# Rotary embedding in a six-layer stage: the halves of a head swapped by a shuffle of partitions on VectorE, in place of a second projection on TensorE

## The reference, cut to what matters

```python
NL, D, H, DFF = (6, 128, 16, 512)
HD = D // H
def _rope(x):
    half = HD // 2
    ...
    x1, x2 = (x[..., :half], x[..., half:])
    return jnp.concatenate([x1 * cos - x2 * sin, x1 * sin + x2 * cos], axis=-1)
for i in range(NL):
    xn = _adaln(x, noise_emb, n1_w[i], n1_b[i])
    qkv = xn @ qkv_w[i].T
    ...
    q = _rope(q.reshape(B, L, H, HD)); k = _rope(k.reshape(B, L, H, HD))
    x = x + _attn(q, k, v, src_mask).reshape(B, L, D) @ so_w[i].T
    xn = _adaln(x, noise_emb, n2_w[i], n2_b[i])
    q = _rope((xn @ cq_w[i].T)...); k = _rope((context @ ck_w[i].T)...); v = (context @ cv_w[i].T)
    x = x + _attn(q, k, v, ctx_mask).reshape(B, L, D) @ co_w[i].T
    ...                     # feed-forward part
```

## Time and profile before

| what | value |
|---|---|
| median of 3 runs | 8145.55 us (8137.73 to 8151.84) |
| the profiled execution's own time | 8119.01 us |
| its span, first to last instruction | 8117.1 us |
| TensorE busy | 6394.4 us (79%) |
| VectorE busy | 5039.5 us (62%) |
| ScalarE busy | 2829.9 us (35%) |
| GpSimd busy | 831.3 us (10%) |
| mean granted TensorE clock | 0.829 |

### The profile page before, as it was taken

One profiled execution on the slowest core, in us unless ns is written; L12 is line 12 of the kernel. 1 busy time (PEld: TensorE's weight loads), 2 busy tenths in 40 slices (PEclk: granted clock), 3 DMA queues, 4 the chain that ended last, 5 costly groups with the idle time before them and its releaser, 6 DMA issues. The chain is left out here.

```text
span 8117.1 us, 210088 instructions
## 1 busy us (share of the span) xinstructions
PE 6394.4 (79%) x89378; PEld 4794.1 (59%) x89401; DVE 5039.5 (62%) x17947; ACT 2829.9 (35%) x4816; POOL 831.3 (10%) x803
## 2 busy tenths in 40 slices
PE   4444589989866698988978868888888888888875
PEld 3333467766643388888856645556556555565653
DVE  6777855455456666666643367577575775756742
ACT  2121133333322311111111135555455554555541
POOL 1114400000000100000000011111110111101100
PEclk7667799999988855555579989999999999999986
DMA  1000000000000000000000000000000000000000
GB/s 31 1 2 1 27 1 1 1 1 1 1 4 0 3 4 4 4 4 4 4 22 0 0 18 2 7 6 2 10 2 4 8 2 10 2 2 10 2 4 10
DMA packets 61243, 45.06 MB, mean 6 GB/s; under 512 B 22521, under 2 KB 56125, under 8 KB 60227
## 3 DMA queue, kind: packets, MB, share of 16 engines
q1 hardware_dynamic: 60355, 32.26, 1.5%
HBM read 30.14 MB, written 2.10 MB: 4 GB/s over the span
## 5 line engine op out<-in xcount | busy, mean ns | idle before, releaser
L368 DVE TENSOR_REDUCE peak<-ps 128x8 f32<-128x1024 f32 (+1 forms) x832 | 816.8, 1023 | 267.1 <-PE ps L290 266.3
L410 ACT ACTIVATE e<-ps,H_lowT_c 77x1024 f32<-77x1024 f32 x384 | 405.6, 1105 | 259.9 <-PE ps L314 259.9
L410 ACT ACTIVATE e<-ps,H_lowT_s 128x1024 f32<-128x1024 f32 x384 | 407.0, 1111 | 248.5 <-PE ps L314 248.5
L328 PEld LDWEIGHTS ps<-e,H_vt 128*32 128x32 f32 (+1 forms) x12288 | 319.8, 112 | 255.5 <-ACT e L410 140.9
L328 PE MATMUL ps<-e,H_vt 128*32 128x128 f32 (+1 forms) x12288 | 432.9, 281 | 23.6 <-DVE xs L388 17.7
L314 PE MATMUL ps<-H_qr,H_km 32*128 32x128 f32 (+1 forms) x12288 | 424.6, 277 | 0.0
L314 PEld LDWEIGHTS ps<-H_qr,H_km 32*128 32x128 f32 (+1 forms) x12288 | 410.2, 170 | 15.4 <-issue 2.2
L1838 PE MATMUL ps<-F_hp,F_encW 128*128 128x1 bf16 (+2 forms) x12288 | 363.4, 166 | 24.7 <-issue 22.4
L1868 PE MATMUL ps<-F_eT,F_ctxp 77*128 77x1 f16 (+1 forms) x12288 | 375.4, 165 | 1.7
L418 ACT ACTIVATE oT<-ps 128x512 f32<-128x512 f32 x416 | 248.4, 597 | 365.9 <-PE ps L328 365.9
L2216 POOL TENSOR_TENSOR H_rstd<-H_veps,neghalf 128x4 f32<-128x4 f32 (+1 forms) x146 | 160.8, 1101 | 2076.3 <-DVE H_veps L2212 2076.3
(11 more groups left out here) (602 smaller groups left out, 14394.4 us busy)
## 6 DMA issues: line engine op xcount, KB each, us to landing
G_w<-in_L_ffn_w SPq DMA_DIRECT2D x16, 256.0 KB
H_f<-in_L_xcond_f_w SPq DMA_DIRECT2D x12, 256.0 KB
H_nw<-in_L_xcond_n_w SPq DMA_DIRECT2D x21, 128.0 KB, 2.1
A_cond<-in_cond SPq DMA_DIRECT2D x1, 2048.0 KB
out_x<-x_all SPq DMA_DIRECT2D x1, 2048.0 KB, 8.7
ctx_rows<-in_ctx SPq DMA_DIRECT2D x1, 1232.0 KB
D_wq<-in_L_xcond_attn_wq SPq DMA_DIRECT2D x2, 512.0 KB
D_wk<-in_L_xcond_attn_wk SPq DMA_DIRECT2D x2, 512.0 KB
```

The source lines that it names most:

```text
L328: last = nc.tensor.matmul(ps[PAD_COLS * s:PAD_COLS * (s + 1), FLAT, r * S:(r + 1) * S], vt_of(u)[0:keys, QUAD * r + s, :], e[0:keys, half, ...
L368: last = nc.vector.tensor_reduce(peak[:, HL * half:HL * (half + 1)], view, AX.X, ALU.max, negate=True)
L410: nc.scalar.activation(e[0:keys, half, :], ps[0:keys, AGAIN[half]:AGAIN[half] + 2, :].rearrange("p b t -> p (b t)"), ACT.Exp, bias=low(u) ...
```

## The change

`rotate` reads one bank instead of two. VectorE first copies the projection out of PSUM with its partitions permuted (a stream shuffle, by the list SWAP, which exchanges partitions 0 to 3 with 4 to 7 within each head of eight, and in the same way in every block of 32), then multiplies the unpermuted projection by the cosine table, waits for the shuffle's own semaphore, and multiplies the permuted copy by the sine table in place. `project` issues one product instead of two, into banks that now alternate with the group, and so waits for the rotation four jobs back instead of two. The four permuted weight matrices, their SBUF tiles and their DMAs are gone (two of the eleven ahead of each layer, two of the eleven within it).

```diff
-                            def project(r, g, i, a, b, src):
+                            def project(r, g, i, m, src):
                                 k, n = job(r, g, i), tokens(r, i)[1]
-                                if g:
-                                    pe.wait_ge(sem["rope_done"], k - 1)
-                                for bank, m in ((2 * i, a), (2 * i + 1, b)):
-                                    last = nc.tensor.matmul(ps[:, bank, 0:n], w[m][:], src, start=True, stop=True)
-                                last.then_inc(sem["q_done"], 1)
+                                if g >= 2:
+                                    pe.wait_ge(sem["rope_done"], k - 3)
+                                nc.tensor.matmul(ps[:, 2 * i + g % 2, 0:n], w[m][:], src, start=True, stop=True).then_inc(sem["q_done"], 1)
...
-                                project(SELF, g, 0, "q_w", "qs_w", xnT2[g % 2][:])
+                                project(SELF, g, 0, "q_w", xnT2[g % 2][:])
...
-                                project(CROSS, g, 1, "ck_w", "cks_w", mine)
+                                project(CROSS, g, 1, "ck_w", mine)
...
                                 if k >= 2:
                                     dve.wait_ge(sem["table_ready"], k - 1)
-                                for bank, table, t in ((2 * i, cosT, ta), (2 * i + 1, sinT, tb)):
-                                    last = nc.vector.tensor_tensor(t[:, k % 2, 0:wide].rearrange("p (u t) -> p u t", u=U),
-                                                                   ps[:, bank, 0:wide].rearrange("p (u t) -> p u t", u=U),
-                                                                   table[:, 0:n].unsqueeze(1).broadcast_to([D, U, n]), ALU.mult)
-                                last.then_inc(sem["rope_done"], 1)
+                                by_batch = lambda t: t.rearrange("p (u t) -> p u t", u=U)
+                                over = lambda table: table[:, 0:n].unsqueeze(1).broadcast_to([D, U, n])
+                                src, kept, swapped = ps[:, 2 * i + g % 2, 0:wide], ta[:, k % 2, 0:wide], tb[:, k % 2, 0:wide]
+                                nc.vector.stream_shuffle(swapped, src, SWAP).then_inc(sem["halves_swapped"], 1)
+                                nc.vector.tensor_tensor(by_batch(kept), by_batch(src), over(cosT), ALU.mult)
+                                dve.wait_ge(sem["halves_swapped"], k + 1)
+                                nc.vector.tensor_tensor(by_batch(swapped), by_batch(swapped), over(sinT), ALU.mult).then_inc(sem["rope_done"], 1)
...
+                        SWAP = [HD * (i // HD) + (i + HD // 2) % HD for i in range(32)]
-                        LATER = 16 * 11
+                        LATER = 16 * 9
```

More of the change, by code:

```diff
@@ L46 @@
     "hid_done", "hid_ready", "ffn_done", "ffn_added", "gate_done", "gate_ready",
-    "upd_done", "upd_ready", "expert_done", "expert_ready", "x_ready", "gram_done",
+    "halves_swapped", "upd_done", "upd_ready", "expert_done", "expert_ready", "x_ready", "gram_done",
     "peaks_turned", "half_peaked", "shift_ready", "again_done", "o_read", "o_flipped",
@@ L2157, in stage_layers @@
                 y_all = sb("H_y", [S, B, D], scope=st)
-                square = ["q_w", "qs_w", "k_w", "ks_w", "v_w", "cqs_w", "cks_w"]
+                square = ["q_w", "k_w", "v_w"]
                 w = {n: sb("H_" + n, [D, D], scope=st) for n in square}
@@ L2261, in first_loads @@
                 def first_loads(l):
-                    out = [(w[n][:], of_layer(l, "L3_" + n, "a p n -> p (a n)")) for n in ("q_w", "qs_w", "k_w", "ks_w", "v_w")]
+                    out = [(w[n][:], of_layer(l, "L3_" + n, "a p n -> p (a n)")) for n in ("q_w", "k_w", "v_w")]
                     for i in range(3):
@@ L2271, in later_loads @@
                     out = [(w[n][:], of_layer(l, "L3_xcond_" + n, "a p n -> p (a n)")) for n in ("so_w", "ck_w", "cq_w", "cv_w", "co_w")]
-                    out += [(w[n][:], of_layer(l, "L3_" + n, "a p n -> p (a n)")) for n in ("cks_w", "cqs_w")]
                     out += [(f2b_raw[:], dram["L3_xcond_f2_b"][bass.ds(l, 1)].rearrange("a n -> (a n)").partition_broadcast(3)),
@@ L2406, in _ @@
                                 pe.wait_ge(sem["xnT_ready"], g + 1)
-                                project(SELF, g, 0, "q_w", "qs_w", xnT2[g % 2][:])
+                                project(SELF, g, 0, "q_w", xnT2[g % 2][:])
                                 if g + 1 < NG:
                                     turn(SELF, g + 1)
-                                project(SELF, g, 1, "k_w", "ks_w", xnT2[g % 2][:])
+                                project(SELF, g, 1, "k_w", xnT2[g % 2][:])
                                 if g == 1:
@@ L2429, in _ @@
                                 pe.wait_ge(sem["xnT_ready"], NG + g + 1)
-                                project(CROSS, g, 0, "cq_w", "cqs_w", xnT2[g % 2][:])
+                                project(CROSS, g, 0, "cq_w", xnT2[g % 2][:])
                                 if g + 1 < NG:
@@ L2808 @@
         arrays["L3_xcond_" + name] = arrays["L3_xcond_" + name].transpose(0, 2, 1)
-    swap = np.arange(D).reshape(NH, 2, HD // 2)[:, ::-1, :].reshape(-1)
     qkv = arrays["L3_xcond_qkv_w"]
     arrays["L3_q_w"], arrays["L3_k_w"], arrays["L3_v_w"] = qkv[:, :, 0:D], qkv[:, :, D:2 * D], qkv[:, :, 2 * D:]
-    arrays["L3_qs_w"] = arrays["L3_q_w"][:, :, swap]
-    arrays["L3_ks_w"] = arrays["L3_k_w"][:, :, swap]
-    arrays["L3_cqs_w"] = arrays["L3_xcond_cq_w"][:, :, swap]
-    arrays["L3_cks_w"] = arrays["L3_xcond_ck_w"][:, :, swap]
-    for name in ("L3_q_w", "L3_qs_w", "L3_k_w", "L3_ks_w", "L3_v_w", "L3_xcond_n1_w", "L3_xcond_n2_w", "L3_xcond_n3_w",
+    for name in ("L3_q_w", "L3_k_w", "L3_v_w", "L3_xcond_n1_w", "L3_xcond_n2_w", "L3_xcond_n3_w",
                  "L3_xcond_n1_b", "L3_xcond_n2_b", "L3_xcond_n3_b"):
```

## The result

The kernel after takes 8171.3 us (median of 10 runs, 8159.6 to 8205.6) against 8142.3 (10 runs, 8119.6 to 8159.3). The ratio is 1.0041, interval 1.0025 to 1.0057: 33 us slower (20 to 46). The profiled execution took 8177.6 us, its span is 8175.8, 58.7 more than the span before. VectorE is busy for 5147.0 us (+107.5), TensorE for 6335.6 (-58.8).

A forecast was written before the change was run, and what follows sets the result against it. SELF was taken as a ring through VectorE and TensorE with VectorE idle 1.27 us a group, CROSS as both full. SELF -1.37 and CROSS +6.74 us a layer gave +32, the clock +18: 8196 us, range 8164 to 8232.

The forecast's parts named there:

- The price of the shuffle: On VectorE, each rotation's added shuffle takes a step of 0.70 us at 512 columns, 0.49 at 308.
- Start: Up to a stretch's first normalisation: 1.70 us a layer gained in SELF, 0.45 lost in CROSS.
- Ring: SELF, first to last normalisation, through VectorE and TensorE in turn: 30.00 us a layer against 28.96, a loss of 1.04.
- Tail: After a stretch's last normalisation: SELF gains 0.47 us a layer, plus about 0.24 for earlier value rows; CROSS loses 0.45.
- Groups: CROSS, first to last normalisation: 26.63 us a layer against 20.79, +5.84, with a group at 5.15.
- The clock: TensorE, less busy, falls to half clock; VectorE waits in three of eight SELF groups: +18 us, bounds 0 and 52.
- The rule against the change: In SELF, the new sine multiplication may have to wait out GpSimd's add: sum 6 us higher, held by the range.
- The clock stays up: Rival: TensorE keeps its clock in both stretches, leaving +32 us, 8178 us; chance 0.14.
- The shuffle apart from its neighbours: Rival: on VectorE the shuffle overlaps no neighbour, a step of 0.90 us: +87 us, 8233 us; chance 0.12.
- the fast copy: Rival: on VectorE the shuffle runs as a fast copy, step 0.35 us: -15 us, 8131 us; chance 0.04.
- Normalisation freed: Rival: normalisation gets out from beside GpSimd's add, step 1.98 to about 1.04 us: -18 us, 8128 us; chance 0.03.
- Half of it: Rival: VectorE has overlooked slack in CROSS, only +10 us, 8156 us; chance 0.05.

The follow-up runs named there:

- g: The kernel after without the shuffle, the sine multiplication reading the projection unpermuted: 8076.5 us against 8138.9 for before, ratio 0.9928.
- b: The kernel before with the shuffle and single product in the SELF projections alone: 8143.9 us against 8138.9 for before, ratio 1.0010.
- c: The kernel before with the shuffle and single product in the CROSS projections alone: 8174.5 us against 8127.4 for before, ratio 1.0056.
- a: The kernel after with two spare products per group on TensorE whose results nobody reads: 8159.8 us, ratio to before 1.0025.
- h1: The kernel after, with GpSimd's add of a group's second rotation waiting for the normalisation of group g+2: 8129.5 us against 8127.4 for before.
- early cosine: The kernel before, each product signalling by itself, so the cosine multiplication begins when the first bank is written: 8096.9 us against 8127.4.
- late add: GpSimd's second add of a group waits for group g+2's normalisation: 8129.5 us on after (h1), 8081.9 on before with early cosine.
- r: The kernel before with early cosine and late add, and q in SELF with one product and a shuffle: 8059.4 us against 8129.3 for before.

## Why the prediction came out as it did

The time lies in the range, and the mechanism is the forecast one. The nearness of the sum is in part luck: a shuffle priced too high made up for terms that were too low.

*What bounds it.* Right. SELF is a ring with time to spare on VectorE; in CROSS both engines were full, VectorE at 3.94 us a group and TensorE at 4.07, and freeing TensorE gave nearly nothing (g, b, c).

*The price of the shuffle.* The mechanism was right, the size off: 0.70 and 0.49 us taken, 0.63 and 0.39 measured (5286.69 to 5287.32, 5524.85 to 5525.24), because its list costs nothing and not 0.08. With 24 shuffles of 512 columns and 7 of 308 that is (24 x 0.07 + 7 x 0.10) x 6 = 14 us too much, the largest error of the sum. The shuffle's duration of 0.73 us is within 0.06 of a multiplication's. By the estimate from the Trainium skill, "VectorE: DVE Perf Modes", "The perf-mode tier table", it would have been a step of 0.71; the measurement decides, and its statement that a shuffle has only the slow rate holds.

*SELF.* Start: 1.71 us earlier taken, 1.66 measured on average. Ring: +1.04 taken; at full clock it is +0.7 (29.67 in a, mean of six, against 28.95). Tail: -0.47 taken, -0.57 at its best (9.57). But k's product at the start runs at half clock and is waited for, 0.67 us at 5289.26, a wait that the sum had excluded; from the first rotation to the first normalisation it is 0.47 us more than before on average, 3 us in six layers. The 0.24 us for earlier value rows were not measured.

*CROSS.* Groups +5.84 taken, +4.92 measured (25.75 against 20.83 on average), all of it the shuffle's size. Start: +0.45 taken. The first rotation begins 0.33 us earlier, and from there to the first normalisation it is 1.19 more: +0.86. Tail: +0.45 taken, +0.65 measured; 0.53 of it, in five of six layers, is the one sine multiplication beside GpSimd's add. Start and tail so make up for most of what the shuffle was priced too high, and CROSS has 38 us where 40 were taken.

*The clock.* 18 us taken, bounds 0 and 52. The ring shows 8.7 us, and the tails, 10.2 on average where 9.57 occur, 4.0 more: 13, and 16 with the wait at the start. The price of one wait was 1.08 in the sum and is 1.10 in the trace. In the groups of CROSS it costs nothing, as forecast. The busy shares that the forecast clock rested on were too low, 56% and 50% of a group, where the windows from first to last normalisation show 65% and 71%: TensorE's busy time grows when it waits between its rows (q's product of a CROSS group is 1.12 us in g, behind a wait, and 1.02 before, back to back). The clock was 0.89 and 0.93 there, and not near 0.67.

*The rule against the change.* The mechanism is measured as foreseen: k's sine multiplication waits for the end of the add, 0.20 us away when it begins in the fifth group of the second layer (0.12 in the sum), and takes 0.74 us where it takes 0.68 without, a step 0.07 longer. It happens in 30 of the 96 rotations of SELF, most of them k's, 2 us, with 6 allowed. It came on top in the tail of CROSS, 3 us, where nothing was allowed. The Trainium skill's "GPSIMD Engine Reference", "1. Specifications", names this form, and the traces of after and h1 bear it out.

*The rivals.* "The clock stays up" is refuted by a SELF clock of 0.82 to 0.89, though its time, 8178, is near the median. The shuffle apart from its neighbours and the fast copy fall with the step of 0.63. "Normalisation freed" did not happen, as argued, since add and normalisation are still released together; h1 shows what it is worth when forced. "Half of it" falls with CROSS groups of 4.99.

*The sum by the measured sizes.* 32 - 14 for the shuffle + 16 for the clock + 2 for the add in SELF + 6 at the start and the tail of CROSS (beyond the shuffle's size) = 42 us, and the traces show 45, where 50 were forecast. The forecast time, 8196 us, was 25 us too long. Of these, 3 are the base, 8142.3 and not 8145.6 us, and 5 are the terms. The rest is that the medians of the timed runs differ by 29 us (by the ratio 33, 20 to 46) and the traces by 45. No run shows where that lies; the upper end of the interval would leave nothing of it.

## What to carry to other kernels

Work moved to another engine costs its full price where that engine sets the pace, and what it leaves behind is a gain only where it was waited for: read both per stretch, not per kernel. Here, on top of early cosine and late add, the same edit pays in one of four rotations, the one that fills a wait (r). Look also at who runs beside a slow instruction and at what a signal waits for: the early cosine gave 30 us and the late add 22 to 32, without a shuffle or beside one, where the edit in its best place gave 26 and as it was made lost 33. And count the start of a stretch, ahead of its first rotation: here it was worth 10 us in SELF.

## What was not expected of the hardware

- The normalisation of four 128x128 tiles takes 1.10 us alone and 2.05 beside GpSimd's add of 128x512, as the prediction had read; h1 shows that the add is the cause, and that all of it is one instruction waiting for the add to end (1.30 us for 0.34). Multiplications from PSUM beside an add keep their 0.68.
- A multiplication of two SBUF tiles that begins during such an add ends a fixed time behind it, 0.33 us at 308 columns and 0.55 at 512. So its price is what is left of the add: 0.46 us become 1.04 when it begins 0.56 into an add of 1.27, and 0.68 become 0.74 when it begins 1.07 into it.
- A VectorE instruction that waits for the one just before it starts 0.13 us later than one that does not.
